# One block of a fused token mixer and mixture-of-experts kernel: the first norm's statistics on ScalarE, merged recurrence steps at other places, weight loads by SyncE, and new orders of four engines

## The chip, the cores and the metric

The kernel runs on one core of a Trainium2 chip. The metric is the device time of one execution in microseconds (us); lower is better. The profile comes from one further execution. Engines are named PE (TensorE), DVE (VectorE), ACT (ScalarE), POOL (GpSimd) and SP (SyncE); a "q" behind a name (SPq, ACTq) is that engine's own instruction queue issuing a transfer.

## The reference, cut to what matters

The input x is (8, 192, 16, 16): 8 images, 192 channels, 256 positions, all float32.

```python
xn = layernorm over channels of x                  # eps 1e-6, "first norm"
q = l2norm(silu(xn @ Wq)); k = l2norm(silu(xn @ Wk)); v = silu(xn @ Wv)
beta = sigmoid(xn @ Wb)                            # 12 heads of 16
# delta rule in chunks of 16 positions, per image and head; S is the 16 x 16 state
#   u_t = beta_t * (v_t - S^T k_t);  S += k_t u_t^T;  o_t = S^T q_t
x1 = x + (xn + o @ Wo)
t  = layernorm over channels of x1                 # eps 1e-5, "second norm"
# router: softmax of 8 logits, two largest kept; 8 experts 192->192->192 (silu gate),
# one shared expert 192->768->192, mixed by a sigmoid gate
out = x1 + alpha * shared(t) + (1 - alpha) * routed(t)
```

## The kernel before, in words

The 256 positions are cut into 16 chunks of 16 positions; a chunk holds 8 x 16 = 128 tokens, one per partition. Work on a chunk falls into stages, and in the code the letter says which: **A** (first norm, projections, l2 norms, scratch writes of k and q), the **recurrence** (no letter), **Fa** (output projection, second norm, router), **Fb** (12 "units" of 192 hidden columns each: up projection on PE, silu and gating on ACT, product on POOL, transposes and down projection on PE) and **Fc** (result back to channel order).

`chunks(step)` runs c from -3 to 18, on every engine. `stage(c, par, d, fn)` runs `fn` for chunk c + d if it exists, so in one turn of the loop the engines hold chunk c's recurrence, chunk c+3's first norm (`A_x`, `A_stats`, `A_var`, `A_bias`, `A_h`), chunk c+2's projections and norms (`A_low`, `A_qk`, `A_vb`, `A_z`, `A_ss`, `A_inv`, `A_khi`, `A_klo`), chunk c-1's second norm and router, and the units of chunks c-2 and c-1. Turns -3 to -1 are the start, before the first recurrence; 16 to 18 are the tail. The order of each engine's work inside a turn is written out by hand, and engines wait for one another by semaphores. Every engine executes its list strictly in order.

The recurrence runs on DVE alone: 64 slots a chunk, four for each of 16 positions (`Pr`, `u`, `bank`, `SH` are their outputs, L1326, L1328, L1330, L1334). A slot is normally two instructions, one for each half of the state (96 elements a partition each), so that the half being read is already finished. A slot in the set `WHOLE` is one instruction of 192 elements. All other DVE work stands behind a slot's number in `others(done)`. PE's `fill` f writes k for two positions into a bank; slot 8f waits for it.

The first norm is formed so: ACT copies x to `xs` (`A_xs`), PE turns it into `bA` (`A_x`), DVE takes `bn_stats` and `bn_aggr` of the bank (`A_stats`, L1063 and L1064) and adds eps (`A_var`, L1074), POOL raises both norms' variances to -0.5 (`rsqrt`, L897), DVE forms the bias (`A_bias`), and ACT writes `h` and `xh` (`A_h`, `A_xh`; `xh` is x + xn). The second norm: PE adds `xh`, by a product with the identity (L398), to the output projection (`Fa_y`, L398 to L400), DVE takes the same statistics of the bank (`Fa_stats`, `Fa_var`), ACT copies the sum over `xh` (`Fa_x1`, L638) and writes `h2` from the bank (`Fa_h`, L644).

k and q go to HBM scratch and come back in another layout: SP issues `scratch_k` (four writes, waiting for `klo` on POOL), `load_k` (two reads, waiting for those writes), `scratch_q`, `spread_q`, in this order for each chunk. Before that SP issues the loads: x of the first four chunks, Wq and Wk, Wo, the router's weights and the up weights' lower rows (`raw1`); ACT issues Wv and Wb, and the up weights' upper rows (`raw0`) behind its first `A_xs`. The up weights are split into high and low parts on ACT (`weights_hi0`, `weights_hi1`) and POOL (`weights_lo0`, `weights_1`), in the turns -2 to 1.

## Time and profile before

| | |
|---|---|
| time, median of 3 runs | 495.12 us (495.06 to 495.85) |
| the profiled execution: its time | 495.17 us |
| the profiled execution: its span | 493.4 us |
| busy share of the span: PE, DVE, ACT, POOL | 86%, 86%, 71%, 83% |
| mean granted clock of TensorE | 0.954 |

The span runs from the first to the last instruction; about 1.8 us of the execution's time lie around it. Busy shares are means over a start, 16 recurrences and a tail, which have different limits. Matmuls are pipelined and their ends are modelled, so a PE that shows as busy may have room; the others' busy times are times of execution.

### The profile page before, as it was taken

To read this page: it belongs to the slowest core of one execution; us is meant where nothing else is said; L and a number is where in the kernel's file an instruction comes from. 1 tells how busy PE (TensorE), PEld (TensorE's weight loads), DVE (VectorE), ACT (ScalarE), POOL (GpSimd) and SP (SyncE) were. 2 spreads that over 40 slices of the span, in tenths; PEclk is the share of its full clock that TensorE was granted. 3 is DMA by queue.
4 is the path that set the end of the run, shared out by engine and by line. 5 is a ranking of instruction groups with operands and counts; after the bars stand their busy time and mean duration, and the time that the engine had idled before them with its cause. 6 is when DMAs were issued, how large, how long until landed. Compare 5 with 4: busy or idle time off the path is not lost.

```text
span 493.4 us, 10463 instructions
## 1 busy us (share of the span) xinstructions
PE 423.7 (86%) x2400; PEld 383.9 (78%) x2400; DVE 422.0 (86%) x2350; ACT 350.9 (71%) x1023; POOL 410.6 (83%) x527
## 2 busy tenths in 40 slices
PE   1344265899999999999999999999999989899996
PEld 0223143889898989898988989898989889899995
DVE  3239899999999999999999999999999999997200
ACT  2795345687877878787868787878786848485872
POOL 5377699989999989898989899998989999895340
PEclk9999555799999999999999999999999999999999
DMA  7958363543233232323233232323222323200301
GB/s 200 219 107 157 98 153 90 137 103 103 70 88 81 79 88 67 103 66 99 71 82 88 82 89 77 94 68 84 79 75 79 82 81 89 88 22 1 113 2 16
DMA packets 45215, 44.10 MB, mean 89 GB/s; under 512 B 20385, under 2 KB 36961, under 8 KB 45153
## 3 DMA queue, kind: packets, MB, share of 16 engines
q1 hardware_dynamic: 41408, 40.87, 32.7%
q10 hardware_dynamic: 3744, 2.57, 1.8%
q8 instruction: 19, 0.31, 0.3%
q14 instruction: 44, 0.35, 0.2%
HBM read 37.13 MB, written 6.29 MB: 88 GB/s over the span
## 4 chain that ended last, share of the span: by engine, by line
DVE 70%; PE 13%; issue 5%; DMA 4%; SPq 4%; ACT 2%; ACTq 1%; POOL 0%; DVEq 0%; POOLq 0%
DVE Pr L1326 15%; DVE bank L1330 15%; DVE u L1328 14%; DVE SH L1334 12%; PE bank L445 2%; DMA k_scratch<-khl 2%; SPq L237 2%; DVE st L1063 1%; PE bank L430 1%; PE bank L418 1%; SPq L272 1%; DVE otok L1170 1%; PE bank L422 1%; PE bank L420 1%; PE bank L421 1%
## 5 line engine op out<-in xcount | busy, mean ns | idle before, releaser
L953 POOL TENSOR_TENSOR hid<-sg,ug 128x192 f32<-128x192 f32 x192 | 111.3, 602 | 20.0 <-ACT ug L688 13.2
L908 POOL TENSOR_TENSOR PQ<-SH,QB 128x768 f32<-128x768 f32 x62 | 112.4, 1835 | 4.3 <-DVE SH L1334 4.3
L1326 DVE TENSOR_TENSOR Pr<-SH,bank 128x96 f32<-128x96 f32 (+1 forms) x467 | 102.6, 256 | 10.1 <-PE bank L385 6.9
L687 ACT ACTIVATE sg<-bank 128x192 f32<-128x192 f32 x192 | 63.5, 331 | 66.0 <-PE bank L422 27.0
L915 POOL TENSOR_TENSOR PQ<-PQ 128x768 f32<-128x768 f32 (+2 forms) x93 | 102.8, 1106 | 6.1
L445 PE MATMUL bank<-Wd,hidT 128*128 128x192 f32 x576 | 107.8, 328 | 0.0
L1330 DVE TENSOR_TENSOR bank<-bank,u 128x96 f32<-128x96 f32 (+1 forms) x452 | 103.7, 268 | 0.1
L1328 DVE TENSOR_REDUCE u<-Pr 128x6 f32<-128x102 f32 (+1 forms) x467 | 103.5, 258 | 0.0
L1334 DVE TENSOR_TENSOR SH<-SH,bank 128x96 f32<-128x96 f32 (+1 forms) x482 | 102.9, 252 | 0.1
L445 PEld LDWEIGHTS bank<-Wd,hidT 128*128 128x128 f32 x576 | 94.8, 190 | 2.4 <-ACT hidT L698 2.4
L418 PE MATMUL bank<-Whi,hiT 128*128 128x384 f32 (+1 forms) x192 | 80.5, 419 | 7.3 <-DVE loT L1104 6.4
L385 PE MATMUL bank<-KR,Sel 128*128 128x384 f32 x128 | 53.5, 421 | 25.0 <-DVE SH L1334 12.4
L421 PE MATMUL bank<-W,hiT 128*128 128x384 f32 (+1 forms) x192 | 66.1, 344 | 0.0
L422 PE MATMUL bank<-W,loT 128*128 128x384 f32 (+1 forms) x192 | 66.1, 344 | 0.0
L420 PE MATMUL bank<-Whi,loT 128*128 128x384 f32 (+1 forms) x192 | 66.0, 344 | 0.0
L419 PE MATMUL bank<-Wlo,hiT 128*128 128x384 f32 (+1 forms) x192 | 65.9, 343 | 0.0
L688 ACT ACTIVATE ug<-bank,gate 128x192 f32<-128x192 f32 x128 | 54.0, 422 | 0.1
L698 ACT ACTIVATE hidT<-bank 128x512 f32<-128x512 f32 (+1 forms) x80 | 44.5, 557 | 10.5 <-PE bank L430 9.4
L385 PEld LDWEIGHTS bank<-KR,Sel 128*128 128x128 f32 x128 | 25.8, 203 | 32.9 <-DVE SH L1334 17.6
L418 PEld LDWEIGHTS bank<-Whi,hiT 128*128 128x128 f32 x192 | 37.0, 193 | 16.2 <-DVE loT L1104 9.8
L722 ACT ACT_TABLE_LOAD x38 | 48.8, 1283 | 0.7
L430 PE MATMUL bank<-ident,hid 128*128 128x128 f32 x288 | 44.7, 273 | 0.0
(144 smaller groups left out, 810.9 us busy)
## 6 DMA issues: line engine op xcount, KB each, us to landing
QB<-q_scratch SPq DMA_DIRECT2D x64, 384.0 KB
k_scratch<-khl SPq DMA_DIRECT2D x64, 48.0 KB, 1.7
KR<-k_scratch SPq DMA_DIRECT2D x32, 96.0 KB, 2.4
q_scratch<-qn SPq DMA_DIRECT2D x64, 24.0 KB, 1.6
Wd<-in_L_ffn_w_down_dram SPq DMA_DIRECT2D x4, 288.0 KB, 8.6
out_dram<-xT SPq DMA_DIRECT2D x1, 896.0 KB, 4.1
Wlo_unsplit<-in_L_ffn_w_gate_dram ACTq DMA_DIRECT2D x1, 768.0 KB, 5.4
Wlo_unsplit<-in_L_ffn_w_up_dram ACTq DMA_DIRECT2D x1, 768.0 KB, 6.5
```

Of the source, the lines that this page charges most:

```text
L385: mm(bKB[f % 2][:, 0:2 * BR * G], Sel[:, f].rearrange("p b x e -> p (b x e)"), KR[:, p, :], start=True, stop=True).then_inc(s_fill, 1)
L418: mm(to, hiT[:, p, 0:P], Whi0[:, w], start=True, stop=False)
L421: mm(to, hiT[:, p, P:2 * P], W1[:, w], start=False, stop=False)
L422: mm(to, loT[:, p, P:2 * P], W1[:, w], start=False, stop=True).then_inc(s_up, 1)
L445: last = mm(bDn[:, 0:C], hidT[:, turn_half(g), k - lo, :], Wd[:, k, :], start=False, stop=(k == KT - 1))
L908: tt(PQ[:, at * BR * HP:(at + n) * BR * HP].rearrange("p (i b h) d -> p i b (h d)", i=n, b=BR), SH[:, lo:lo + n].rearrange("p i b h d -> p ...
L915: chained(tt(PQ[:, :, 0:w], PQ[:, :, 0:w], PQ[:, :, w:2 * w], ALU.add))
L953: tt(hid[:, r * H:(r + 1) * H], sg[:, m % RING], ug[:, m % RING], ALU.mult).then_inc(s_hid, 1)
L1326: v = each(slot, lambda lo, hi: count(tt(Pr[:, lo:hi, i, :, 0:D], prev[:, lo:hi], KB[:, lo:hi], ALU.mult)), Sb)
L1328: v = each(slot + 1, lambda lo, hi: count(nc.vector.tensor_reduce(u[:, i % 2, lo:hi], Pr[:, lo:hi, i], X, ALU.add, negate=True)), v)
L1330: v = each(slot + 2, lambda lo, hi: count(tt(KB[:, lo:hi], KB[:, lo:hi], u[:, i % 2, lo:hi].unsqueeze(3).to_broadcast([P, hi - lo, HP, D]) ...
L1334: ins = tt(SH[:, i, lo:hi], prev[:, lo:hi], KB[:, lo:hi], ALU.add)
```

## The change

1. The first norm's statistics move from DVE to ACT. `A_stats` is now two passes over the bank: a copy with scale -1/192 whose row sum is minus the mean, and a square with that sum as bias whose row sum is 192 times the variance. `A_var` on DVE multiplies and adds eps; `A_bias` loses its sign.
2. The second norm's sum is formed on DVE (`Fa_add`, bank + `xh` into `xh`); the identity product in `Fa_y` and `Fa_x1` on ACT go, and the statistics and `Fa_h` read `xh` in SBUF.
3. `Fa_stats`, `A_low`, `Fa_split` and `Fa_max` are cut into smaller steps, placed anew; `WHOLE` has 13 slots in place of 12.
4. `raw0` is loaded by SP, ahead of the rest of the weights; Wo and the bias come last. The first chunk's `scratch_k` and `load_k` are issued by ACT in turn -2.
5. In the turns before 1, ACT loads the silu table just before `A_silu_v`, not behind `A_inv`. In the steady turns it runs the router's exponential and `A_xh` ahead of `A_inv`.
6. PE, ACT and POOL have new orders in every turn.

```diff
-WHOLE = frozenset((28, 32, 37, 38, 49, 50, 51, 54, 55, 56, 57, 58))
+WHOLE = frozenset((11, 24, 35, 47, 48, 49, 50, 51, 54, 55, 56, 57, 58))
...
+            if later(a, 1):
+                eng.wait_ge(s_fill, max(a * 8 - 8, 1))
+            for br in range(BR):
...
+                load_up(sp, 0, raw0, 0, C0)
+                load_router(sp, 0, raw0[:, :], 0, C0)
+                load_up(sp, 1, raw1[0:C1], C0, C)
+                load_up(sp, 1, raw1[C1:P], C0, C)
+                load_router(sp, 1, raw1[0:C1], C0, C)
+                load_router(sp, 1, raw1[C1:P], C0, C)
                 sp.dma_start(Wo0[:, :], Wo[0:C0, :]).then_inc(s_wo, 16)
                 sp.dma_start(Wo1[:, :], Wo[C0:C, :]).then_inc(s_wo, 16)
-                load_router(sp, 0, raw0[:, :], 0, C0)
-                load_router(sp, 1, raw1[0:C1], C0, C)
-                load_router(sp, 1, raw1[C1:P], C0, C)
...
-                at(1, scratch_k)
-                at(1, load_k)
+                if c >= 0:
+                    at(1, partial(scratch_k, sp))
...
-                mm(bFa[:, 0:C], ident[:, :], xh[:, bass.ds(f, 1), :].rearrange("p z c -> p (z c)"), start=True, stop=False)
-                mm(bFa[:, 0:C], oc0[:, :], Wo0[:, :], start=False, stop=False)
-                mm(bFa[:, 0:C], oc1[:, :], Wo1[:, :], start=False, stop=True).then_inc(s_y, 1)
+                project(bFa[:, 0:C], oc0[:, :], oc1[:, :], Wo0[:, :], Wo1[:, :]).then_inc(s_y, 1)
...
                     at(3, A_qk)
                 elif c < NC:
-                    at(-3, Fb_down, 4)
+                    at(0, fill, 3)
                     at(-2, Fb_up, 5)
-                    at(0, fill, 3)
-                    at(-3, Fc_out)
                     at(-2, Fb_up, 6)
                     at(3, A_x)
                     at(-1, Fa_o)
+                    at(-3, Fb_down, 4)
+                    at(-1, Fa_y)
+                    at(-2, Fb_turn, 0)
                     at(0, fill, 4)
-                    at(-2, Fb_turn, 0)
                     at(-2, Fb_up, 7)
-                    at(-1, Fa_y)
                     at(-2, Fb_up, 8)
+                    at(0, fill, 5)
+                    at(-2, Fb_up, 9)
+                    at(-3, Fc_out)
                     at(-2, Fb_turn, 1)
-                    at(-2, Fb_up, 9)
+                    at(-1, Fa_h)
                     at(-2, Fb_up, 10)
-                    at(0, fill, 5)
-                    at(-1, Fa_h)
-                    at(-2, Fb_turn, 2)
+                    at(-2, Fb_up, 11)
                     at(0, fill, 6)
-                    at(-2, Fb_up, 11)
                     at(-1, Fb_up, 0)
                     at(-2, Fb_down, 0)
+                    at(-2, Fb_turn, 2)
                     at(0, fill, 7)
+                    at(-1, Fb_up, 1)
+                    at(3, A_h)
                     at(-2, Fb_down, 1)
-                    at(-1, Fb_up, 1)
                     at(1, fill, 0)
                     at(-2, Fb_down, 2)
                     at(-2, Fb_turn, 3)
-                    at(3, A_h)
+                    at(1, fill, 1)
                     at(-1, Fb_up, 2)
                     at(-1, Fb_up, 3)
                     at(-2, Fb_turn, 4)
-                    at(1, fill, 1)
                     at(-2, Fb_down, 3)
+                    at(1, fill, 2)
                     at(-1, Fb_up, 4)
...
+            def A_stats(a, p):
+
+                act.wait_ge(s_xT, a + 1)
+                if later(a, 1):
+                    act.wait_ge(s_nm1, a)
+                    act.wait_ge(s_ve1, a)
+                chained(f(dev[:, :], bA[:, 0:C], ACT.Copy, scale=-1.0 / C, accum_out=mv1[:, 0:1]))
+                f(dev[:, :], bA[:, 0:C], ACT.Square, bias=mv1[:, 0:1], accum_out=mv1[:, 1:2]).then_inc(s_dev, 1)
+
             def A_plus(a, p):
...
-            def Fa_x1(q, p):
-                act.wait_ge(s_ve2, q + 1)
-                f(xh[:, bass.ds(q, 1), :].rearrange("p z c -> p (z c)"), bFa[:, 0:C], ACT.Copy).then_inc(s_x1, 1)
-
             def Fa_h(q, p):
                 act.wait_ge(s_nm2, q + 1)
                 if later(q, 1):
                     act.wait_ge(s_h2Tp, q)
-                f(h2[:, :], bFa[:, 0:C], ACT.Identity, scale=rstd2[:, 0:1],
+                f(h2[:, :], xh[:, bass.ds(q, 1), :].rearrange("p z c -> p (z c)"), ACT.Identity, scale=rstd2[:, 0:1],
                   bias=nmr2[:, 0:1]).then_inc(s_h2, 1)
...
                     once(c, 0, weights_hi1, 3)
+                    if 0 <= c + 2 < NC:
+                        table(0, SILU)
                     at(2, A_silu_v)
...
+                    once(c, -1, weights_hi0, 5)
+                    at(3, A_stats)
                     once(c, -1, weights_hi0, 6)
                     at(2, A_sq)
+                    once(c, -1, weights_hi0, 7)
+                    table(c + 2, LN_EXP)
+                    at(2, A_inv)
+                    at(3, A_plus)
+                    at(3, A_h)
+                    at(3, A_xh)
+                    at(2, A_khi)
+                    once(c, -2, scratch_k, act, 0, 0)
+                    once(c, -2, load_k, act, 0, 0)
+                    once(c, 0, weights_hi1, 5)
+                    once(c, -1, weights_hi0, 8)
+                    at(3, A_hT)
...
+                    at(-2, unit, 10)
+                    at(-2, hidden, 1)
+                    at(-3, Fc_out)
+                    at(3, A_plus)
+                    at(-2, unit, 11)
+                    at(3, A_h)
+                    table(c - 1, LN_EXP)
+                    at(-1, Fa_exp)
+                    at(3, A_xh)
                     table(c + 2, LN_EXP)
                     at(2, A_inv)
                     table(0, SILU)
-                    once(c, 0, weights_hi1, 5)
-                    at(3, A_plus)
-                    once(c, -1, weights_hi0, 7)
-                    at(3, A_h)
-                    at(3, A_xh)
-                    once(c, -1, weights_hi0, 8)
+                    at(-2, hidden, 2)
+                    at(-1, unit, 0)
+                    at(3, A_hT)
+                    at(-1, unit, 1)
...
+                    once(c, -1, weights_lo0, 5)
                     if c <= NC:
                         rsqrt(c)
...
                 elif c < NC:
+                    at(-2, hidden, 6)
                     once(c, 1, weights_1, 8)
-                    at(-2, hidden, 6)
-                    once(c, 1, weights_1, 9)
-                    at(-2, hidden, 7)
                     if c <= NC:
                         rsqrt(c)
+                    once(c, 1, weights_1, 9)
                     once(c, 1, weights_1, 10)
                     once(c, 1, weights_1, 11)
                     at(0, reading, 0)
+                    at(-2, hidden, 7)
                     at(-2, hidden, 8)
                     at(-2, hidden, 9)
+                    at(0, summing, 0)
                     at(-2, hidden, 10)
-                    at(0, summing, 0)
+                    at(2, A_qn)
                     at(-2, hidden, 11)
...
                 return s_chain, n[0]
-            def stats(src, st, mv):
-                dve.wait_ge(*count(nc.vector.bn_stats(st[:, :], src)))
-                return count(nc.vector.bn_aggr(mv[:, :], st[:, :]))
-
-            def A_stats(a, p):
-                dve.wait_ge(s_xT, a + 1)
-                w["mv1"] = stats(bA[:, 0:C], st1, mv1)
-
             def A_var(a, p):
-                dve.wait_ge(*w["mv1"])
+                dve.wait_ge(s_dev, a + 1)
                 if later(a, 1):
                     dve.wait_ge(s_rs, a)
-                ts(ve[:, 0:1], mv1[:, 1:2], 1e-6, None, ALU.add).then_inc(s_ve1, 1)
+                ts(ve[:, 0:1], mv1[:, 1:2], 1.0 / C, 1e-6, ALU.mult, ALU.add).then_inc(s_ve1, 1)
             def A_bias(a, p):
                 dve.wait_ge(s_rs, a + 1)
                 if later(a, 1):
                     dve.wait_ge(s_h, a)
                     dve.wait_ge(s_xh, a)
-                ts(nmr1[:, :], mv1[:, 0:1], rstd1, -1.0, ALU.mult, ALU.mult).then_inc(s_nm1, 1)
+                ts(nmr1[:, :], mv1[:, 0:1], rstd1, None, ALU.mult).then_inc(s_nm1, 1)
+
+            def Fa_add(q, p):
+                row = xh[:, bass.ds(q, 1), :].rearrange("p z c -> p (z c)")
+                dve.wait_ge(s_y, q + 1)
+                w["x1"] = count(tt(row, bFa[:, 0:C], row, ALU.add))
             def Fa_stats(q, p):
-                dve.wait_ge(s_y, q + 1)
-                w["mv2"] = stats(bFa[:, 0:C], st2, mv2)
+                dve.wait_ge(*w["x1"])
+                w["st2"] = count(nc.vector.bn_stats(st2[:, :], xh[:, bass.ds(q, 1), :].rearrange("p z c -> p (z c)")))
+
+            def Fa_mean(q, p):
+                dve.wait_ge(*w["st2"])
...
+            def Fa_logits(q, p):
+                dve.wait_ge(s_up, q * UN + 1)
+                w["logit"] = count(nc.vector.tensor_copy(logit[:, :], bUp[0][:, 0:E]))
+
             def Fa_max(q, p):
...
+                        at(19, 2, A_z)
+                        at(31, 1, A_vT)
+                        at(40, 3, A_var)
+                        at(51, 2, A_ss)
+                        at(51, 3, A_bias)
                     elif c < NC:
-                        at(7, 2, A_low)
-                        at(17, 2, A_z)
+                        at(10, 2, A_low)
+                        at(11, 2, A_low_tail)
+                        at(20, 2, A_z)
                         at(23, -1, Fa_otok)
-                        at(27, 3, A_stats)
-                        at(28, 1, A_vT)
-                        at(31, 3, A_var)
-                        at(32, -1, Fa_stats)
-                        at(32, -1, Fa_var)
-                        at(36, -1, Fa_bias)
-                        at(37, 2, A_ss)
-                        at(38, 3, A_bias)
-                        at(43, -1, Fa_split)
-                        at(48, -1, Fa_max)
+                        at(24, 1, A_vT)
+                        at(30, -1, Fa_add)
+                        at(30, -1, Fa_stats)
+                        at(30, -1, Fa_mean)
+                        at(30, 3, A_var)
+                        at(30, -1, Fa_var)
+                        at(34, -1, Fa_bias)
+                        at(35, 2, A_ss)
+                        at(42, -1, Fa_split)
+                        at(42, -1, Fa_split_tail)
+                        at(46, 3, A_bias)
```

The semaphore counts that go with the cut steps are left out, and so are the tail's orders; the same kinds of moves are made there.

## Rows read from the trace of the kernel before

**Rows 1.** Windows: busy time of each engine in a stretch, clock, DMA share.
```profile
60.50:88.40 27.90, 16.70 (x47) 11.61 (x47) 25.82 (x146) 15.01 (x42) 25.34 (x28) 0.50 0.51 118
114.50:373.10 258.60, 252.52 (x1502) 232.50 (x1501) 255.41 (x1452) 205.82 (x621) 240.44 (x301) 1.00 0.30 83
```

**Rows 2.** Timeline of DVE, one steady chunk (c = 7): start, duration, instruction.
```profile
217.60 0.42 DVE L1326 TENSOR_TENSOR Pr<-SH,bank 128x96 f32<-128x96 f32 x2
217.94 0.42 DVE L1328 TENSOR_REDUCE u<-Pr 128x6 f32<-128x102 f32 x2
...
226.02 0.37 DVE L1170 STREAM_TRANSPOSE otok<-oT 128x192 f32<-128x192 f32 x1
...
227.60 0.36 DVE L1063 BATCH_NORM_STATS2 st<-bank 128x6 f32<-128x192 f32 x1
...
228.09 0.34 DVE L1326 TENSOR_TENSOR Pr<-SH,bank 128x192 f32<-128x192 f32 x1
...
229.59 0.15 DVE L1074 TENSOR_SCALAR ve<-mv 128x1 f32<-128x1 f32 x1
229.81 0.36 DVE L1326 TENSOR_TENSOR Pr<-SH,bank 128x192 f32<-128x192 f32 x1
230.08 0.36 DVE L1063 BATCH_NORM_STATS2 st<-bank 128x6 f32<-128x192 f32 x1
...
230.76 0.41 DVE L1328 TENSOR_REDUCE u<-Pr 128x6 f32<-128x102 f32 x2
...
237.14 0.16 DVE L1174 COPY logit<-bank 128x8 f32<-128x8 f32 x1
237.22 0.16 DVE L1175 TENSOR_REDUCE negmax<-bank 128x1 f32<-128x8 f32 x1
237.41 0.23 DVE L1183 TENSOR_TENSOR bank<-bank,logit 128x64 f32<-128x64 f32 x1
```

**Rows 3.** Timeline of POOL in the same chunk: its one idle time.
```profile
231.10 0.70 POOL L897 TENSOR_TENSOR rs<-ve,neg_half 128x2 f32<-128x2 f32 x1 [1.00 <-DVE ve L1091]
```

**Rows 4.** Timeline of ACT and of PE around Fa_y in the same chunk.
```profile
227.10 0.26 ACT L634 ACTIVATE oc<-bank 64x128 f32<-64x128 f32 x1
```
```profile
228.22 0.49 PE L398 MATMUL bank<-xh,ident 128*128 128x192 f32 x2
...
228.97 0.59 PE L400 MATMUL bank<-Wo,oc 64*128 64x192 f32 x2
```

**Rows 5.** Groups of ACT's instructions, shapes apart: count, busy, mean ns, idle before.
```profile
L644 ACT ACTIVATE h<-bank,nmr,rs 128x192 f32<-128x192 f32 x16 | 8.2, 515 | 5.3 <-DVE nmr L1097 5.3
```

**Rows 6.** Timeline of ACT in the start.
```profile
10.37 0.29 ACT L566 ACTIVATE rstd<-rs,one 128x1 f32<-128x1 f32 x1 [3.74 <-issue]
...
20.11 1.28 ACT L722 ACT_TABLE_LOAD   x1
...
23.48 0.26 ACT L580 ACTIVATE hhi<-bank 128x128 fp32r<-128x128 f32 x1
...
28.99 0.52 ACT L603 ACTIVATE sq<-qk 128x384 f32<-128x384 f32 x1
```

**Rows 7.** Timeline of SP's queue in the start: issues of the first two chunks' k.
```profile
23.50 1.76 SPq L237 DMA_DIRECT2D k_scratch<-khl  x4
30.56 1.20 SPq L253 DMA_DIRECT2D KR<-k_scratch  x2
...
43.89 7.40 SPq L237 DMA_DIRECT2D k_scratch<-khl  x4
```

**Rows 8.** DMA issues by line: size of one, median us from issue to landing.
```profile
k_scratch<-khl SPq DMA_DIRECT2D x64, 48.0 KB, 1.7
```

**Rows 9.** Timeline of DVE: its waits around the first recurrence.
```profile
34.42 0.42 DVE L1326 TENSOR_TENSOR Pr<-SH,bank 128x96 f32<-128x96 f32 x2 [4.21 <-PE bank L385]
...
44.41 0.42 DVE L1326 TENSOR_TENSOR Pr<-SH,bank 128x96 f32<-128x96 f32 x2 [1.14 <-PE bank L385]
...
60.53 0.42 DVE L1326 TENSOR_TENSOR Pr<-SH,bank 128x96 f32<-128x96 f32 x2 [1.54 <-PE bank L385]
```

More of the change, by code:

```diff
@@ new lines, in step @@
+                    at(3, A_hT)
+                    once(c, -1, weights_hi0, 9)
+                    once(c, -1, weights_hi0, 10)
+                    once(c, -2, weights_hi0, 0)
+                    once(c, -1, weights_hi0, 11)
+                    once(c, -2, weights_hi0, 1)
+                    once(c, -1, weights_hi1, 0)
+                    once(c, 0, weights_hi1, 6)
+                    once(c, -1, weights_hi1, 1)
+                elif c < NC:
+                    if c == 1:
+                        table(0, SILU)
+                    at(-2, unit, 3)
+                    at(-2, unit, 4)
+                    at(3, A_xs)
+                    at(2, A_silu_qk)
+                    once(c, 1, weights_hi1, 7)
+                    at(2, A_silu_v)
+                    at(0, place, 1)
+                    at(-2, unit, 5)
+                    at(-1, Fa_oc)
+                    at(3, A_stats)
+                    at(-3, Fc_res)
+                    at(-2, unit, 6)
+                    once(c, 1, weights_hi1, 8)
+                    at(-2, hidden, 0)
+                    once(c, 1, weights_hi1, 9)
+                    at(2, A_sq)
+                    at(-2, unit, 7)
+                    at(-2, unit, 8)
+                    once(c, 1, weights_hi1, 10)
+                    once(c, 1, weights_hi1, 11)
+                    at(-1, Fa_h)
+                    at(-2, unit, 9)
+                    at(1, place, 0)
+                    at(-1, Fa_hT)
+                    at(-2, unit, 10)
+                    at(-2, hidden, 1)
+                    at(-3, Fc_out)
+                    at(3, A_plus)
[4 more added lines that the diff above has]
+                    at(3, A_xh)
@@ L757, in step @@
-                    once(c, -1, weights_hi0, 10)
-                    once(c, -1, weights_hi0, 11)
-                    once(c, -1, weights_hi1, 0)
-                    once(c, -1, weights_hi1, 1)
-                elif c < NC:
-                    at(3, A_xs)
-                    at(-2, unit, 3)
-                    at(-2, unit, 4)
-                    once(c, 1, weights_hi1, 7)
-                    at(2, A_silu_qk)
-                    at(2, A_sq)
-                    at(-3, Fc_res)
-                    once(c, 1, weights_hi1, 8)
-                    at(0, place, 1)
-                    once(c, 1, weights_hi1, 9)
-                    at(2, A_silu_v)
-                    at(-2, unit, 5)
-                    at(-1, Fa_oc)
-                    at(-2, hidden, 0)
-                    at(-2, unit, 6)
-                    at(-2, unit, 7)
-                    at(1, place, 0)
-                    at(-3, Fc_out)
-                    once(c, 1, weights_hi1, 10)
-                    at(-2, unit, 8)
-                    once(c, 1, weights_hi1, 11)
-                    at(-1, Fa_x1)
-                    at(-2, hidden, 1)
-                    at(-1, Fa_h)
-                    at(-2, unit, 9)
-                    at(3, A_plus)
-                    at(-1, Fa_hT)
-                    at(-2, unit, 10)
-                    at(-2, unit, 11)
-                    table(c + 2, LN_EXP)
-                    at(2, A_inv)
-                    table(c - 1, LN_EXP)
-                    at(-1, Fa_exp)
-                    table(0, SILU)
-                    at(3, A_h)
-                    at(-2, hidden, 2)
-                    at(3, A_xh)
-                    at(-1, unit, 0)
-                    at(-1, unit, 1)
@@ L1276, in others @@
                     else:
-                        at(-1, -1, Fa_otok)
-                        at(0, -1, Fa_stats)
-                        at(24, -1, Fa_var)
-                        at(44, -1, Fa_bias)
-                        at(47, -1, Fa_split)
-                        at(48, -1, Fa_max)
+                        at(1, -1, Fa_otok)
+                        at(10, -1, Fa_add)
+                        at(20, -1, Fa_stats)
+                        at(23, -1, Fa_mean)
+                        at(26, -1, Fa_var)
+                        at(26, -1, Fa_bias)
+                        at(28, -1, Fa_split)
+                        at(28, -1, Fa_split_tail)
+                        at(41, -1, Fa_logits)
+                        at(47, -1, Fa_max)
                         at(48, -1, G_dif, done)
```

146 lines of the change are left out of this document (69 added, 77 removed).

## The prediction

> **What bounds the kernel now.** I read the stages first [rows 1]: ten steady chunks take 258.60 us, and DVE is busy for 255.41 of them. No other engine is so full for a reason of its own, so the steady period is the length of DVE's list: the 64 slots and what stands behind them. A chunk is 25.86 us there. The chunk c = 1 takes 27.9 at half clock, 2.0 more than a steady one. Then I read one steady chunk of DVE [rows 2] for the distance from one start to the next, which is the price of an instruction in the list. A slot in two halves costs 0.33 (217.60 to 217.94), a merged slot 0.27 (229.81 to 230.08), an instruction on a few elements 0.08 (237.14 to 237.22). POOL has one idle microsecond in that chunk, waiting for a variance that DVE delivers [rows 3]; its work is then 25.8 - 1.0 = 24.8 us a chunk, the floor under any gain on DVE. In the start DVE waits for PE's first fill until 34.42, in the first recurrence 1.14 more, and before the second 1.54 [rows 9]; both fills that open a recurrence wait for k to come back from HBM [rows 7].
>
> **The steady chunk, on DVE.** `A_stats` goes: 227.60 to 228.09, -0.49. The group of `A_var` and the second norm's statistics took 229.59 to 229.81 and 230.08 to 230.76, thus 0.22 + 0.68. Now `A_var` stands between `bn_aggr` and `Fa_var`, where DVE waits for the aggregate anyway: -0.22. `Fa_add` is new and the statistics wait for its end; nearest row, a two-input instruction of 192 elements with a bank as input, 0.36 long [rows 2], with about 0.02 to start the dependent one: +0.38. Bounds: 0.27, were its end not waited for, to 0.5. Logits and maximum took 0.27 until the difference table could start (237.14 to 237.41); now a merged slot covers the wait and they cost 2 x 0.08: -0.11. One slot more is merged: -0.06. `A_bias` now precedes a merged slot, as `A_var` did, and a merged slot behind a half-slot wants some 0.2 between them where a small step gives 0.1: +0.08. Sum -0.42. `A_low` in two pieces costs what it did, since each piece is one of the two instructions. `Fa_stats` reads SBUF in place of a bank, and I count nothing for it (bounds -0.05 and +0.05).
>
> What can take this back is lateness. The statistics stood 12.48 us into the chunk. `Fa_add` comes 0.60 (two slots), 0.49 (`A_stats`), 0.22 (`A_var`) and 0.06 (merging) earlier: 11.11 us in. The sum from PE ended at 228.97 + 0.59 = 229.56, 11.96 in; unchanged it would stall DVE 0.85 a chunk, twice the gain. It comes sooner for two reasons. `oc` was ready at 227.36 and the product began at 228.22 [rows 4], because PE did a fill, a transpose group and an up projection between them; of these `Fb_down` 4 alone remains, and it runs while `oc` is copied. The identity product (228.22 to about 228.55) is gone. That is -0.8 and -0.33: the sum ends 10.8 to 11.1 us in. The cover is therefore 0 to 0.3 us, and I take 0.06 of stall. The same holds for what follows: bias at slot 34, `Fa_h`, transpose, split at slot 42 have about half a microsecond.
>
> ACT gets two passes over a bank in place of `Fa_x1`. The nearest row is a pass with two per-partition operands, 0.515 [rows 5]; below, a 128-column pass of 0.26 [rows 4]. So 0.5 to 1.0 us is added and one pass removed, with 205.82 busy of 258.60 [rows 1], thus 5.3 us idle a chunk. They stand behind `oc` and ahead of `res`, unit 6 and the first `hidden`, which PE and POOL wait for; POOL's product of unit 6 then starts just about when its idle microsecond began, so nothing is late. Later in the turn `A_h`, the exponential, `A_xh` and the four passes of `A_inv` run before the silu table and `hidden` 2, so the third down group, the transposes and units 2 and 3 come about 1 us later than now. PE had room there; the next thing late is `Fa_o`, and I find it at 9.0 us in, beside a transpose `otok` that ends at 8.7 (226.02 + 0.37 less the origin 217.60, and 0.06). It is in the 10.8 to 11.1 above. POOL has the same work, with unit 7 behind the products: 24.8 under a period of 25.4, enough.
>
> Net -0.36 a chunk, over the 11 chunks c = 2 to 12: -4.0 (range -6 to 0). The last three chunks have no first norm: a merged slot 11 with nothing behind it costs what `Fa_max` gives; -0.3 together. The chunk c = 1 should lose most of its 2.0 us of waits, since PE reaches `Fa_y` and the split comes a slot sooner: -1.6 (0 to -2.2).
>
> **The start.** ACT began the first `A_plus` at 10.37 after 3.74 us of issue [rows 6]; the four `raw0` loads are gone from its queue, so it starts when the power is there, -0.8. Then two statistics passes stand ahead of `A_sq`, +0.9: nothing gained up to `A_inv`. Behind it the table load of 1.28 at 20.11 leaves the way of `khi`, and the four writes start at 22.4 in place of 23.50, now from ACT. There they wait less, perhaps. They were issued by 25.26 and landed by 30.56 [rows 7], where a write of this size takes 1.7 at the median [rows 8], since the weights were ahead of them in SP's queue. On ACT's queue bounds are 24.2 + 1.7 = 25.9 and the same 30.5. I take 27.5, nearer the first, because only transfers already running stand ahead of them, but these fill the engines.
>
> In the Trainium skill, "DMA: Bandwidth & Descriptors", section "Issuing engines are not separate DMA queues", transfers of all issuing engines run on the same 16 engines and interleave, and another issuer saves issue time alone. By that rule the writes would land near 30; by its section on queues, which lets an engine alternate between issuers' rings, near 27. The row at 30.56 is of one queue and agrees with either.
>
> But ACT executes in order. From 22.4 it issues four writes (1.76), waits until 27.5, issues two reads (1.20), and only at 28.7 goes on to the second chunk's `A_hT`, which began at 23.48 [rows 6]: +5.3. Its squares were done at 29.51; now +5.3, +1.28 (the silu table stands there now), +0.9 (third chunk's statistics), about 37.0. DVE must sum them (0.5) before it may start the first recurrence in its list, so that starts at 37.6 and not 34.42: +3.2, although k is there by 32. Against it: the second chunk's k was issued at 43.89, behind SP's x load, and DVE waited 1.54 for it; SP no longer waits for the first k, so that is gone. The wait of 1.14 for a fill shrinks to some 0.5, and `A_stats` (0.49) leaves the first recurrence, and slots are fewer by 0.1. That is -2.8: the second recurrence starts at 60.9 where it started at 60.53, +0.4. Each microsecond of k's landing moves this by one: -1.6 at 25.9, +3 at 30.5.
>
> **The tail** is a full list of PE; it loses the identity product, -0.3.
>
> **Sum**: +0.4 - 1.6 - 4.0 - 0.3 - 0.3 = -5.8. The profiled execution took 495.17 (span 493.4 and 1.8 around it), 0.05 above the median of the runs, which changes nothing: 489.4 us.
>
> **Rivals.** *A: the first k writes overtake nothing* and land near 30. The busy queue speaks for it, the separate issuer against. +2.5 to +3: 492.2. Chance 0.13.
>
> *B: the second norm's sum is late.* If `Fa_y` ends at 12.0 us into the chunk as it does now, or later because `hidden` 2, behind the second table load, holds PE's third down group, DVE stalls 0.9 in each of 12 chunks: +10.8, 500. It ends above the kernel before once the sum is more than 0.5 us later than I put it (5.8 / 12). For it: the cover of 0 to 0.3. Against it: the order by which PE now does nothing between `oc` and `Fa_y`. Typical price +8: 497.5. Chance 0.12.
>
> *C: another engine holds the period*, POOL most likely: its one idle microsecond must suffice for `rsqrt` waiting on slot 30, the product of unit 6 and of unit 7. With 0.3 of new waits a chunk it sits at 25.7 and DVE's gain is idle time; only c = 1 and the tail are left, with the start even: 493.5 to 495. Chance 0.10.
>
> *D: the start goes well*: k lands at 26 and ACT's chain is 1 us shorter than I have it: 487. Chance 0.15.
>
> The forecast has 0.50. A measurement of this kernel can tell about 0.2%, 1 us, from no change. Faster by over 1 us (below 494.1): forecast, A, D, and half of C, less a little: 0.81. Within: 0.07. Slower: all of B, 0.12. The range goes from 486.0 (D with a full steady gain) to 494.8 (A and C), and leaves out B.
>
> **What the profile after would show.** Steady starts of `Pr` 25.4 us apart, where they are 25.8. No `bn_stats` of `bA`; `Fa_add` with no idle time before it, else B. POOL's idle time at `rs` some 0.6. ACT: k writes at 22.4, reads at 27.5 (A: 30), `hhi` at 28.7. DVE's first `Pr` at 37.6, released by the squares and not by PE; first `Pr` of the second chunk near 61. If the first recurrence starts before 35, my account of ACT's blocked queue is wrong; if steady chunks take 25.8 with DVE idle, the gain was real but hidden.

## The result and the profile after

| | median us | range | runs |
|---|---|---|---|
| before | 494.01 | 493.02 to 495.85 | 20 |
| after | 495.50 | 494.56 to 496.51 | 20 |

The ratio is 1.0027, with a 95% interval from 1.0017 to 1.0037: the change made the kernel slower by 1.5 us. I had forecast 489.4, faster.

The two profiled executions don't show this by themselves. Before's took 495.17, 1.2 above its median, and after's 494.58, 0.9 below. So both kernels were traced once more: before at 493.50 (span 491.7), after at 495.22 (span 493.5), each within 0.6 of its median. The account uses this second pair. Stretches run from the first `Pr` of a recurrence to the next, and the tail from DVE's `PQ` behind the last one to the span's end.

| stretch | before | after | difference | predicted |
|---|---|---|---|---|
| up to the second recurrence | 59.00 | 63.75 | +4.75 | +0.4 |
| c = 1 | 27.82 | 27.81 | 0.0 | -1.6 |
| c = 2 to 12 | 284.60 | 281.43 | -3.17 | -4.0 |
| c = 13 to 15 | 75.08 | 75.43 | +0.35 | -0.3 |
| tail | 45.24 | 45.06 | -0.2 | -0.3 |
| sum | 491.74 | 493.48 | +1.7 | -5.8 |

**The steady chunk** is shorter, as planned. The windows of after (the columns of [rows 1]), ten chunks:

```profile
116.42:372.22 255.80, 246.08 (x1482) 228.61 (x1481) 253.86 (x1432) 211.93 (x651) 241.19 (x301) 1.00 0.30 83
```

They took 258.60 before. The timeline of DVE in one of them (c = 8, origin 244.18), the answer to [rows 2]:

```profile
255.33 0.35 DVE L1088 TENSOR_TENSOR xh<-bank,xh 128x192 f32<-128x192 f32 x1
255.72 0.36 DVE L1092 BATCH_NORM_STATS2 st<-xh 128x6 f32<-128x192 f32 x1
256.11 0.18 DVE L1096 BATCH_NORM_AGGREGATE mv<-st 128x2 f32<-128x6 f32 x1
256.21 0.14 DVE L1076 TENSOR_SCALAR ve<-mv 128x1 f32<-128x1 f32 x1
256.33 0.15 DVE L1102 TENSOR_SCALAR ve<-mv 128x1 f32<-128x1 f32 x1
...
263.39 0.16 DVE L1198 COPY logit<-bank 128x8 f32<-128x8 f32 x1
263.46 0.16 DVE L1202 TENSOR_REDUCE negmax<-bank 128x1 f32<-128x8 f32 x1
```

`Fa_add` costs 0.39 and starts 11.15 us into the chunk with no idle time in front of it. On PE, in the same chunk (the answer to [rows 4]), the product starts 0.05 after `oc` is copied, where it started 0.86 after it before. It ends at 255.15, which is 10.97 us in:

```profile
253.73 0.26 ACT L642 ACTIVATE oc<-bank 64x128 f32<-64x128 f32 x1
```

```profile
254.04 0.59 PE L335 MATMUL bank<-Wo,oc 128*128 128x192 f32 x2
254.56 0.59 PE L336 MATMUL bank<-Wo,oc 64*128 64x192 f32 x2
```

**The start** is where the time went. ACT's timeline of after, the answer to [rows 6] and to the first two lines of [rows 7]:

```profile
16.27 0.33 ACT L566 ACTIVATE dev<-bank 128x192 f32<-128x192 f32 x1
16.61 0.20 ACT L566 ACTIVATION_READ_ACCUMULATOR dev<-bank 128x1 f32 x1
16.84 0.42 ACT L567 ACTIVATE dev<-bank,mv 128x192 f32<-128x192 f32 x1
17.16 0.19 ACT L567 ACTIVATION_READ_ACCUMULATOR dev<-bank,mv 128x1 f32 x1
...
22.50 2.03 ACTq L236 DMA_DIRECT2D k_scratch<-khl  x4
30.72 1.24 ACTq L245 DMA_DIRECT2D KR<-k_scratch  x2
32.08 0.28 ACT L588 ACTIVATE hhi<-bank 128x128 fp32r<-128x128 f32 x1 [10.70 <-issue]
```

The writes were issued by 24.53, 0.7 sooner than before, yet the reads (`KR` is k as read back) go out at 30.72, as late as before's 30.56. Until then ACT stands, and the second chunk's `hhi` (ACT's copy of the transposed norm, from which the projections start) comes at 32.08 in place of 23.48. DVE's timeline, the answer to [rows 9]:

```profile
32.82 0.29 DVE L1129 TENSOR_TENSOR hlo<-bank,hhi 128x128 fp32r<-128x128 f32 x1 [14.26 <-ACT hhi L590]
...
40.12 0.55 DVE L1162 TENSOR_REDUCE ss<-sq 128x24 f32<-128x384 f32 x1 [0.67 <-ACT sq L611]
...
40.70 0.41 DVE L1362 TENSOR_TENSOR Pr<-SH,bank 128x96 f32<-128x96 f32 x2
...
49.69 0.42 DVE L1362 TENSOR_TENSOR Pr<-SH,bank 128x96 f32<-128x96 f32 x2 [0.44 <-PE bank L388]
...
63.94 0.41 DVE L1362 TENSOR_TENSOR Pr<-SH,bank 128x96 f32<-128x96 f32 x2
```

What held the k writes shows in the queues' packets by stretches of time (packets, MB, share of the 16 engines). q1 is SP's queue, q10 ACT's. First 22 to 24 us of after, then 26 to 27, then 27 to 28:

```profile
q1 hardware_dynamic: 518, 0.38, 112.4%
...
q1 hardware_dynamic: 277, 0.18, 113.7%
...
q1 hardware_dynamic: 531, 0.09, 78.4%
q10 hardware_dynamic: 304, 0.11, 49.5%
```

From 22.5 to 27 no packet of ACT's queue runs, though its first write was issued at 22.50. SP had handed over the 2.4 MB of `raw1` ahead of it, and its queue moves 0.84 MB in these 4.5 us. Whether the writes waited inside the DMA engines or on the way to them, no trace shows.

### The profile page after: what moved, and what is told of

It reads as the page before. It is cut to its first block, busy times and chain, and to the rows that moved or that the text cites. A ratio compares the mean times of both kernels' runs of the same rounds, so it can differ in the third digit from the quotient of the medians.

```text
span 492.8 us, 10462 instructions
## 1 busy us (share of the span) xinstructions
PE 414.5 (84%) x2368; PEld 376.9 (76%) x2368; DVE 418.9 (85%) x2319; ACT 360.6 (73%) x1071; POOL 411.9 (84%) x527
## 4 chain that ended last, share of the span: by engine, by line
DVE 73%; PE 11%; issue 6%; ACT 1%; DVEq 0%; ACTq 0%
DVE Pr L1362 17%; DVE u L1364 16%; DVE bank L1366 16%; DVE SH L1370 12%; PE bank L444 2%; DVE ss L1162 2%; DVE st L1092 1%; PE bank L418 1%; PE bank L422 1%; PE bank L420 1%; PE bank L421 1%; PE bank L419 1%; DVE xh L1088 1%; DVE loT L1114 1%; PE bank L430 1%
## 5 line engine op out<-in xcount | busy, mean ns | idle before, releaser
L963 POOL TENSOR_TENSOR hid<-sg,ug 128x192 f32<-128x192 f32 x192 | 112.6, 603 | 30.5 <-ACT ug L692 20.9
L1364 DVE TENSOR_REDUCE u<-Pr 128x6 f32<-128x102 f32 (+1 forms) x482 | 104.6, 255 | 0.1
L444 PEld LDWEIGHTS bank<-Wd,hidT 128*128 128x128 f32 x576 | 93.0, 190 | 13.6 <-ACT hidT L702 13.6
L1370 DVE TENSOR_TENSOR SH<-SH,bank 128x96 f32<-128x96 f32 (+1 forms) x437 | 100.5, 264 | 0.8 <-issue 0.2
L388 PE MATMUL bank<-KR,Sel 128*128 128x384 f32 x128 | 55.4, 436 | 20.4 <-DVE SH L1370 20.4
L418 PE MATMUL bank<-Whi,hiT 128*128 128x384 f32 (+1 forms) x192 | 70.3, 366 | 1.8 <-DVE loT L1120 1.6
L702 ACT ACTIVATE hidT<-bank 128x512 f32<-128x512 f32 (+1 forms) x80 | 44.5, 557 | 14.7 <-PE bank L430 13.9
L388 PEld LDWEIGHTS bank<-KR,Sel 128*128 128x128 f32 x128 | 26.2, 205 | 25.9 <-DVE SH L1370 21.2
```

The source lines that it names most:

```text
L388: mm(bKB[f % 2][:, 0:2 * BR * G], Sel[:, f].rearrange("p b x e -> p (b x e)"), KR[:, p, :], start=True, stop=True).then_inc(s_fill, 1)
L418: mm(to, hiT[:, p, 0:P], Whi0[:, w], start=True, stop=False)
L444: last = mm(bDn[:, 0:C], hidT[:, turn_half(g), k - lo, :], Wd[:, k, :], start=False, stop=(k == KT - 1))
L963: tt(hid[:, r * H:(r + 1) * H], sg[:, m % RING], ug[:, m % RING], ALU.mult).then_inc(s_hid, 1)
L1364: v = each(slot + 1, lambda lo, hi: count(nc.vector.tensor_reduce(u[:, i % 2, lo:hi], Pr[:, lo:hi, i], X, ALU.add, negate=True)), v)
L1370: ins = tt(SH[:, i, lo:hi], prev[:, lo:hi], KB[:, lo:hi], ALU.add)
```

## The experiments

Steady chunks repeat from trace to trace: chunks c = 3 to 14 together took 308.9 and 308.8 in the two traces of before, and 306.4, 306.3, 306.5 and 306.4 in after's two, `k_on_sp` and `reads_on_sp`. So a trace tells 0.1 to 0.2 us there. Medians tell less: before's own lay between 493.90 and 494.66 in five groups of runs, so differences of less than about 0.8 between variants need a trace.

**Two more traces.**

> The kernel before once more, for a second trace: the one at hand took 495.17, 1.2 above the median of its 20 runs, and 12 steady chunks of four variants agree within 0.1 us from trace to trace. Theory: what differs from execution to execution lies ahead of the second recurrence, so that an execution of 494 starts it near 59.4 in place of 60.53, and chunks c = 3 to 14 take 308.9 again. Rival: the steady chunks scatter, and the comparison of two traces there is worth little.

It took 493.50. The second recurrence began at 59.00, and c = 3 to 14 took 308.80. The difference to the first trace, 1.67, is 1.53 of start: here the second chunk's k was read back at 54.56, 1.7 sooner than at 56.28 in the first. As expected.

> The kernel after once more, for a second trace: the one at hand took 494.58, 0.9 below the median of its 20 runs. Theory: the scatter lies ahead of the second recurrence here too, in when the first k has come back; an execution of 495.5 starts the second recurrence near 64.9 in place of 63.94, and chunks c = 3 to 14 take 306.4 again. With it the start costs 5 in the median and not 3.4, which turns the sign. Rival: start at 63.9 again, and the time lost in the steady part or the tail.

It took 495.22, with the second recurrence at 63.75: not later, and the theory on the scatter fell for this kernel. The time is in c = 1, 27.81 long where it was 26.50. DVE's timeline, first of the trace of after, then of the second one:

```profile
75.73 0.36 DVE L1088 TENSOR_TENSOR xh<-bank,xh 128x192 f32<-128x192 f32 x1 [0.56 <-PE bank L336]
```

```profile
76.85 0.36 DVE L1088 TENSOR_TENSOR xh<-bank,xh 128x192 f32<-128x192 f32 x1 [1.88 <-PE bank L336]
```

And PE's product ahead of it, again the first trace and then the second:

```profile
74.61 0.56 PE L335 MATMUL bank<-Wo,oc 128*128 128x192 f32 x2 [0.61 <-ACT oc L642]
75.10 0.59 PE L336 MATMUL bank<-Wo,oc 64*128 64x192 f32 x2
```

```profile
74.90 0.98 PE L335 MATMUL bank<-Wo,oc 128*128 128x192 f32 x2 [0.61 <-ACT oc L642]
75.81 1.00 PE L336 MATMUL bank<-Wo,oc 64*128 64x192 f32 x2
```

The same matmuls take 1.7 times as long. In c = 1 they took 0.98 and 1.00 or 1.01 in `reads_on_sp`, `stats_on_dve`, `raw1_half_late`, `fewer_merges` and `all_three` too, and 0.98, 0.85, 1.01 for the three steps in both traces of before. The first trace of after was the exception, with `k_on_sp` (0.56 and 0.79) beside it.

**The start undone.** Before's load order, its orders up to c = 0, and k on SP, with the two passes kept:

```diff
-                    once(c, -2, scratch_k, act, 0, 0)
-                    once(c, -2, load_k, act, 0, 0)
+                    once(c, -3, load_up, act, 0, raw0, 0, C0)
...
-                if c >= 0:
-                    at(1, partial(scratch_k, sp))
+                at(1, partial(scratch_k, sp))
```

> The kernel after with the start of the kernel before: its load order (first weight block on ACT's queue), its orders of the chunks up to c = 0 on every engine, and the first k written and read by SP; the first norm's two passes on ACT stay, ahead of the squares. From c = 1 on it is the kernel after. Theory (the start gave the steady gain back): the two traces lie 3.4 us apart at the second recurrence (63.94 against 60.53) and in the other direction by 4.0 behind it, so this kernel should start its second recurrence near 60.5 to 61.5 and take 491 to 492.5. Rival (the steady list is no shorter in most executions, and the traces chosen mislead): 494.5 to 495.5.

492.38 us (492.24 without the disturbed execution), ratio to before 0.9948 (0.9929 to 0.9968), as expected. The profiled execution was the disturbed one (a span of 1040 us), so only the times of the other six count. With the old start the rest of the change gains 2.3 to 2.4 us; so the new start gives it back.

**k alone back on SP.** Both `once` lines of k go from ACT, and SP's guard `if c >= 0` goes.

> The kernel after with one thing undone: the first chunk's four k writes and two k reads go back to SP's queue, behind its loads. Theory (ACT stands 10.7 us behind its own k read, and with it the second chunk's copies, table loads and squares): ACT takes up hhi near 22 in place of 32.08, the first Pr is then released by PE's fill near 35, the second recurrence starts near 60.5 to 61.5 in place of 63.94, and the time is 492 to 493. Rival (the new order of ACT's start, passes and table loads, is what is late, wherever k is issued): second recurrence still near 63.5, 495.

492.27 us, 0.9959 (0.9942 to 0.9975). ACT took up `hhi` at 22.43, the first `Pr` started at 35.14 and the second recurrence at 60.37. It is within 0.1 of the time of the whole start undone, so no cost of the new orders in the start shows (the times of either variant scatter by 3 us), and moving k back recovers 3.2 us.

**The reads alone on SP.**

```diff
-                    once(c, -2, load_k, act, 0, 0)
...
                 at(1, scratch_q)
+                if c == -1:
+                    load_k(sp, 0, 0)
```

> The kernel after with only the two reads of the first k on SP's queue, behind its q writes; the four k writes stay on ACT. Theory (the wait ahead of the reads holds ACT, not the issuing of the writes): ACT goes on at 24.6, k is in SBUF as now (reads issued near 30.7), first Pr near 34.5, second recurrence near 60 to 61, time 491.5 to 492.5, up to 0.8 below the variant with all six on SP, whose writes are issued about 3 us later. Rival (k's landing alone sets the start): first Pr still past 40, no change, 495.5.

490.07 us, 0.9911 (0.9893 to 0.9928), faster than both kernels and than I expected. From its trace, ACT, SP and DVE:

```profile
25.15 0.28 ACT L590 ACTIVATE hhi<-bank 128x128 fp32r<-128x128 f32 x1 [3.39 <-issue]
```

```profile
31.23 1.22 SPq L245 DMA_DIRECT2D KR<-k_scratch  x2
```

```profile
35.10 0.42 DVE L1363 TENSOR_TENSOR Pr<-SH,bank 128x96 f32<-128x96 f32 x2 [1.24 <-PE bank L390]
...
58.31 0.42 DVE L1363 TENSOR_TENSOR Pr<-SH,bank 128x96 f32<-128x96 f32 x2
```

k comes no sooner, and the first `Pr` starts 5.6 sooner: the wait in ACT's list was the cost, not k. In `k_on_sp` the writes were issued 2.5 later, at 25.36, and the reads still went out at 31.08: issuing k early bought nothing there. I had allowed 0.8 between the two variants and found 2.2. 2.06 of that lies ahead of the second recurrence, which started at 58.31: in `k_on_sp` DVE waited 1.92 for the fill before it (its k was read back at 55.31), here not at all (54.02).

**The same part alone in the kernel before.** The six transfers of the first k behind `A_khi` on ACT, all orders as before. (`load_k` also takes over after's wait for a fill.)

> The kernel before with one part of the change alone: the first chunk's four k writes and two k reads issued by ACT, right behind the rounding of k; all orders are those of before. Theory (ACT executes in order, and the k writes sit behind weights in the DMA engines until about 30, whoever issued them): ACT takes up the second chunk's hhi near 31.5 to 32 in place of 23.48, its squares follow 8 us later near 37.5, the first Pr starts near 38.5 to 39 in place of 34.42, the second recurrence near 62 to 63 in place of 60.53, and the time is 496 to 497. Rival (issuing from ACT is harmless in the order of before, where the silu table is loaded ahead of the wait): within 0.5 of the kernel before.

501.25 us, 1.0144 (1.0121 to 1.0167), 4 more than I expected. ACT stood from 25.1 to 32.46, its `hhi` came at 34.79, and the sum of the squares was ready near 41.5. The rest is k: the two reads took up to 10.5 us to land (2.4 to 2.6 in before). The first line is of before, the second of this kernel, both the DMA landing times of `KR` in the start:

```profile
DMA to landing us min/median/max: 2.4/2.5/2.6
```

```profile
DMA to landing us min/median/max: 5.3/7.9/10.5
```

From 34 to 44 us q10 has 6 to 129 packets in each 2 us beside SP's queue, which then carried q's spreading and the rest of x. So the first `Pr` waited for PE's fill until 44.36, 2.85 longer than for the squares. In after the same reads took 2.4 us. What differs is the order of issue: there they went out at 30.72, 1.2 ahead of q's spreading, here at 32.46, 0.2 behind it; `raw1_late`, below, shows the same, but no run changes the order alone. SP's timeline (`QB` is q as spread), first of after, then of this kernel:

```profile
31.90 2.75 SPq L267 DMA_DIRECT2D QB<-q_scratch  x4
```

```profile
32.25 2.62 SPq L266 DMA_DIRECT2D QB<-q_scratch  x4
```

**Fewer weights ahead of k.** All of `raw1` behind q's spreading:

```diff
-                load_up(sp, 1, raw1[0:C1], C0, C)
...
                 at(1, spread_q)
                 if c == -1:
+                    load_up(sp, 1, raw1[0:C1], C0, C)
...
```

> The kernel after with the second block of expert weights (2.4 MB: gate, up, router rows from 128 to 191) loaded by SP behind the first q's spreading, in place of ahead of the first k. ACT still issues k and waits for it. Theory (the k writes wait behind weights that the DMA engines hold already: packets of ACT's queue ran only from 27.0 on, though issued from 22.5): with the engines empty the writes land near 26.3, the reads are issued then, hhi at 27.7 in place of 32.08, first Pr near 36.5, second recurrence near 60, time 491.5. Rival A (a k write takes that long on ACT's queue whatever else runs): landing near 30.7, no change. Rival B (the late weights then hold POOL, which splits them inside the first recurrence, and DVE waits for POOL): first Pr early, but waits of DVE on QB, on the reads of the states or on norms in the first recurrence; 494 to 496.

505.22 us, 1.0216 (1.0196 to 1.0236). Both halves of the question were answered. ACT's timeline:

```profile
22.97 1.80 ACTq L236 DMA_DIRECT2D k_scratch<-khl  x4
26.02 1.23 ACTq L245 DMA_DIRECT2D KR<-k_scratch  x2
27.38 0.28 ACT L588 ACTIVATE hhi<-bank 128x128 fp32r<-128x128 f32 x1 [5.53 <-issue]
...
59.39 0.94 ACT L681 ACTIVATE hid<-W_unsplit 64x394 fp32r<-64x394 f32 x2 [16.17 <-DMA W_unsplit<-in_L_ffn_sg_w_dram]
```

Without `raw1` ahead of them the writes landed by 26.0, at the 25.9 of my lower bound. But the reads issued there, 1.2 behind q's spreading (24.83), landed late beside it and the weights, and ACT then waited 16.17 for the weights. The landing times of `KR` in its start:

```profile
DMA to landing us min/median/max: 5.9/9.4/12.9
```

So PE's first fill came late, the first `Pr` started at 40.39, and the first recurrence lasted 34.07. I had expected 491.5. Rival B of this run was right in that the late weights held the first recurrence: POOL waited 15.57 behind ACT, and DVE stood 8.43 us, until 60.82. The price was higher, and the first `Pr` not early.

With only half of `raw1` late, and the reads on SP:

> The variant with only the two k reads on SP (490.1), with half of the second weight block (partitions 64 to 127, 1.2 MB) loaded by SP behind the reads of the first k. Theory (the k writes wait for the weights that SP has handed over before them): with 1.2 MB less ahead the backlog ends near 25, the reads are issued near 27 in place of 31.23, and the first Pr comes as early as the squares let it, 33.5 to 34 in place of 35.10: 489 to 489.8. Rival (the late half is then late for ACT, which reads it first at 39.8, behind q's spreading of 1.5 MB): first Pr early, but ACT waits for the weights, norms come late in the first recurrence, 491 to 495.

489.23 us, 0.9887 (0.9866 to 0.9908), as expected. Reads at 25.85, first `Pr` at 33.35 and no wait, second recurrence at 56.55. Of the 1.76 gained there 0.42 went in c = 1, which took 28.51.

**The first norm's statistics back on DVE**, in the variant of 490.07:

```diff
+                        at(27, 3, A_stats)
                         at(30, -1, Fa_add)
```

> The variant with only the two k reads on SP (490.1), with the first norm's statistics undone: bn_stats and bn_aggr on DVE at slot 27, ahead of A_var, and no passes on ACT. Theory (DVE's list is the period): a steady chunk is 0.49 longer, 25.95 in place of 25.45, 12 chunks give +5.9, less what ACT's free 1.0 us a chunk gives back in the start (squares 0.9 sooner) and in c = 1: 494.5 to 496. Rival (the two passes on ACT cost elsewhere what they save on DVE): less than +3.

493.56 us, 0.9987 (0.9975 to 0.9998), thus +3.5, between my 494.5 and the rival's bound of +3. Ten steady chunks took 260.06 in place of 255.84: +0.42 each, where I had 0.49. The two passes do pay on ACT.

**x added by PE**, no `Fa_add`:

```diff
-                project(bFa[:, 0:C], oc0[:, :], oc1[:, :], Wo0[:, :], Wo1[:, :]).then_inc(s_y, 1)
+                mm(bFa[:, 0:C], ident[:, :], xh[:, bass.ds(f, 1), :]...)
+                mm(bFa[:, 0:C], oc0[:, :], Wo0[:, :], start=False, stop=False)
...
-                        at(30, -1, Fa_add)
```

> The variant with only the two k reads on SP (490.1), with the second norm's sum undone: x is added by PE's identity product again, ACT copies the sum to SBUF, and Fa_add is gone from DVE; slots and merges as they are. Theory (Fa_add costs DVE 0.39 a chunk, and the sum has a cover of about 0.2): the identity product makes the sum 0.33 later, 11.3 us in, where the statistics now ask for it at 11.15; stall 0.15 to 0.2, net -0.2 a chunk over 12, and in the last three chunks -0.3 each; PE's tail +0.1: 487 to 488.5. Rival (PE and ACT, with 0.33 and 0.25 more a chunk, make what follows late, as the transposes and the split at slot 42): no gain or a loss, 490 to 493.

491.30 us, 0.9935 (0.992 to 0.995): +1.2, the rival's number. DVE's waits in ten steady chunks:

```profile
DVE st L1104 <- PE bank L406: 5.5, 10, 0.7
```

DVE saves 0.39 a chunk and stalls 0.55: a chunk is 25.74 in place of 25.58. One step of the product more, and in the chunk that starts at 162.52 the sum ends at 174.24, 11.72 us in, where I had 11.3. So the mechanism is the stall that I had named, three times as long, and not the late transposes of the rival. It is rival B of the prediction at work. The last three chunks, where I had -0.3 each, gained nothing (75.47 in place of 75.50).

**The empty merges undone** in the last two chunks:

```diff
+                            whole = slot in WHOLE and c >= 1 and not (c >= NC - 2 and slot in (11, 35) or c == NC - 1 and slot == 24)
```

> The variant with only the two k reads on SP (490.1), with the five merged slots that have nothing behind them in the last chunks (slots 11 and 35 of c = 14 and 15, slot 24 of c = 15) in two halves again. By the trace of after such a slot costs 0.39 where two halves cost 0.33. Theory: -0.06 each, chunk 14 at 25.05 and chunk 15 0.18 shorter, in all -0.3: 489.8. Rival (the merge costs nothing there): 490.1. What the last three chunks lose otherwise, +0.39 a chunk for Fa_add with no statistics of the first norm to take away, stays.

488.51 us, 0.9871 (0.9849 to 0.9893), 1.56 below its base. The last two chunks took 24.77 and 24.40 in place of 25.18 and 24.89, so 0.18 for each merge, three times the price I had. DVE's timeline of after around slot 11 of c = 14 shows why:

```profile
400.65 0.42 DVE L1364 TENSOR_REDUCE u<-Pr 128x6 f32<-128x102 f32 x2
400.99 0.42 DVE L1366 TENSOR_TENSOR bank<-bank,u 128x96 f32<-128x96 f32 x2
401.51 0.35 DVE L1370 TENSOR_TENSOR SH<-SH,bank 128x192 f32<-128x192 f32 x1
401.90 0.42 DVE L1362 TENSOR_TENSOR Pr<-SH,bank 128x96 f32<-128x96 f32 x2
```

A half-slot ahead of the merge takes 0.52 in place of 0.34, since the merge needs both of its halves, and the merge itself 0.39. A small step has to stand on either side. Of the remaining 0.66 of this run, 0.32 lies in the tail and 0.27 in the start; one trace of each doesn't say why.

**All three edits.**

> The kernel after with three edits together: the two reads of the first k on SP's queue, half of the second weight block behind them, and the five empty merges of the last chunks in halves. Theory (the three work in different places: ACT's queue, the load order, DVE's last list): their gains add up. The trace with the late half starts c = 3 at 110.56, 1.2 ahead of the trace with the merges undone (111.77), which ended its span at 486.8: 485.6 and 1.8 around it, 487.4; from the medians 490.07 - 0.84 - 1.56 = 487.7. Rival (the earlier start only makes the second chunk wait longer, since PE and POOL still split weights in c = 1): 488.3 to 488.6, no better than with the merges alone.

488.25 us, 0.9885 (0.9868 to 0.9901). The gains don't add up to the 487.4 to 487.7 that I expected; the time is at the edge of the rival's 488.3 to 488.6. The second recurrence began at 57.12, 0.9 sooner than with the merges alone, but c = 1 took 28.25 in place of 27.81, and c = 3 began at 111.09, 0.7 sooner. The medians, 488.25 and 488.51, are too near to rank. Against before, measured beside each of them, they are 5.7 and 6.0 us less.

## Why the prediction was wrong

**The steady chunk** was right in mechanism and near in size. It is 0.29 a chunk for c = 2 to 12, forecast 0.36. `Fa_add`, the variances and the cover came out as computed: the sum 10.97 us in, forecast 10.8 to 11.1, and no stall. The mis-sized term is `A_stats`: -0.49 as the distance of two rows, but 0.42 when put back. (The 0.06 of stall that didn't come is lost again in terms that no run separates.) Rival C is refuted, since the period fell and POOL followed; but POOL's wait for the variance is 0.1 to 0.4 a chunk, not 0.6. Rival B did not happen, and `x1_by_pe` shows how near it was.

**The start: the step that failed is "I take 27.5"** for k's landing. It was 30.7, rival A, which I gave 0.13. The rest of the working held: by it ACT goes on at 32, the first `Pr` comes at 40.8 and the second recurrence at 64.1; the trace has 32.08, 40.70 and 63.94. The start by rival A was then +3.6, and the first trace of after has +3.4. The ground on which I chose, that only running transfers stand ahead of another queue's, was wrong here: ACT's writes had no packet for 4.5 us while SP's queue moved what it had been handed before, and without `raw1` there they landed by 26.0. With this term alone put right the sum would have been 492.6; the rest of the miss is c = 1 (1.6), the steady chunks (0.8) and the last three (0.65). The rule of the Trainium skill, "DMA: Bandwidth & Descriptors", section "Issuing engines are not separate DMA queues", by which the issuer saves issue time alone, agrees with the 30.72. Its section "Queues, rings and completion order", by which an engine takes turns between queues by packets, agrees with the shared stretches behind 27, and not with the 4.5 us in which q10 had no packet beside a busy q1.

The other 1.3 of the start's +4.75 is the base. I worked against a profiled execution that three runs put near the median; over 20 runs it was 1.2 above. It held a wait of 1.54 for the second k that before's second trace doesn't have (60.53 against 59.00), and I booked its removal as a gain. The time before falls by 1.2 with it, so it moves the start's row and hardly the sum.

**The chunk c = 1: -1.6 forecast, 0.0 found.** In the second pair the sum from PE comes sooner, 13.1 us into the chunk where it came at 13.9, but DVE asks for it at 11.2 where it asked at 13.5. The wait for it grew from 0.49 to 1.88; that for `otok`, 0.85, is gone; all waits together are 2.26 against 1.83. I let the waits shrink with PE's order, did not put the earlier demand against them, and did not price the product at the speed that it has in c = 1. In after's first trace, where the product was fast, c = 1 took 26.50, near my 26.2; that was luck of one execution.

**The last three chunks: -0.3 forecast, +0.35 found.** The gain of the first norm's statistics isn't there to be had, as I wrote, but `Fa_add` still takes its 0.39 of DVE's list in each, which I forgot, and five merges stand empty at 0.18 each, of which I counted only those at slot 11 and made them even with `Fa_max`.

**The tail** gave 0.2 of 0.3.

## What to carry over

Moving a transfer's issue to another engine moves its waits too: ask what stands behind the wait in that engine's list before asking how much sooner the data may come. Here a write queued behind megabytes of weights landed when these were through, whoever issued it, so put the load behind the write, and not all of it. A small read that goes out just ahead of another queue's large transfers landed in 2.4 us, and just behind them in up to 12.9. And where a list gets shorter, what it waits for doesn't: compare the new time of demand with the time of supply, in each stage by that stage's durations.

## What the runs showed of the hardware

ACT's summing pass is followed by an instruction of its own that reads the accumulator. The groups of after (count, busy, mean ns):

```profile
L567 ACT ACTIVATE dev<-bank,mv 128x192 f32<-128x192 f32 x16 | 6.7, 421 | 0.5
L566 ACT ACTIVATE dev<-bank 128x192 f32<-128x192 f32 x16 | 5.1, 321 | 1.5 <-PE bank L349 1.5
L566 ACT ACTIVATION_READ_ACCUMULATOR dev<-bank 128x1 f32 x16 | 3.2, 198 | 0.0
L567 ACT ACTIVATION_READ_ACCUMULATOR dev<-bank,mv 128x1 f32 x16 | 3.1, 193 | 0.0
```

The two passes take 0.98 us in the start (16.27 to 17.25), near the upper bound that I had, and 0.86 in a steady chunk (253.88 to 254.74).

Two queues didn't share evenly here. ACT's writes had no packet for 4.5 us beside SP's weights (after), and its small reads took 5.3 to 12.9 us to land beside SP's larger transfers (`before_k_act`, `raw1_late`), 2.4 alone (after).

The product of c = 1 ran at 0.98 and 1.00 us in most traces and at 0.56 and 0.59 in one. In the second trace of after the granted clock reads 1.00 (2.4 GHz) in the windows from 74 to 78 us, and in `fewer_merges`, with the same durations, 0.50 (1.2 GHz). The two traces of before say the same: c = 1 took 27.83 with the clock at 0.50 and 27.82 with it at 1.00. So the recorded clock doesn't explain the durations, nor the 2.0 us of c = 1 that the prediction set beside a half clock, and why they differ stays open.
